# Plain attention: the maximum of a half is turned two periods sooner, and a third bank goes to turned tiles from period 9 on

## The reference

```python
energy = jnp.einsum('nhqd,nhkd->nhqk', q, k)
attn = jax.nn.softmax(energy / jnp.sqrt(jnp.float32(hd)), axis=3)
out = jnp.einsum('nhql,nhld->nhqd', attn, v)
```

## Time and profile before

| | us |
|---|---|
| median of 3 runs | 1981.02 (1980.35 to 1981.33) |
| the profiled execution | 1978.19 |
| its span, first to last instruction | 1976.4 |
| plain attention, first reduce to last output | 1011.4 to 1713 |
| reduces L1241, 512 | 590.8 busy |
| exponentials L1275, 1024 | 556.3 busy |
| turned tiles L1147, 1024 | 341.1 busy |

### The profile page before, as it was taken

The page is one execution under the profiler, slowest core; times in us unless marked ns, Lnnn a source line. Parts: engine busy times, 40 slices in busy tenths (PEclk is TensorE's granted clock), DMA queues, the critical chain, the costliest instruction groups (busy, mean ns, idle before and its releaser), DMA issues. The chain is left out here.

```text
span 1976.4 us, 40754 instructions
## 1 busy us (share of the span) xinstructions
PE 1741.5 (88%) x15061; PEld 901.7 (46%) x15061; DVE 1399.7 (71%) x3172; ACT 1151.1 (58%) x2314; POOL 581.1 (29%) x817
## 2 busy tenths in 40 slices
PE   5699999999999968799659999999999999687895
PEld 2356666666666545476312222222232332255563
DVE  6676766767788356542569999999899998656431
ACT  3336666666656632222328898989888887432231
POOL 2312122221122146677440000003310000167774
PEclk9779999999999978879768999999999998689888
DMA  5642744454540053232230000000000000062334
GB/s 162 162 84 50 129 90 78 96 98 72 92 89 12 23 150 60 34 59 36 77 127 9 28 18 18 24 29 18 18 18 24 28 3 23 17 171 38 60 40 84
DMA packets 108005, 120.95 MB, mean 61 GB/s; under 512 B 14360, under 2 KB 72960, under 8 KB 107808
## 3 DMA queue, kind: packets, MB, share of 16 engines
q1 hardware_dynamic: 83616, 100.97, 21.7%
q0 software_dynamic: 24192, 17.38, 6.4%
HBM read 81.71 MB, written 35.65 MB: 59 GB/s over the span
## 5 line engine op out<-in xcount | busy, mean ns | idle before, releaser
L1241 DVE TENSOR_REDUCE mx<-wide 128x2 f32<-128x1024 f32 x512 | 590.8, 1218 | 44.8 <-PE wide L1154 43.4
L1275 ACT ACTIVATE pT<-bank 128x512 f32<-128x512 f32 x1024 | 556.3, 595 | 89.5 <-PE bank L1147 79.1
L903 ACT ACTIVATE pT<-bank 128x512 f32<-128x512 f32 (+3 forms) x768 | 344.0, 490 | 238.8 <-PE bank L757 229.9
L1147 PE MATMUL bank<-q_st,k_st 51*128 51x512 bf16 x1024 | 341.1, 395 | 14.9 <-ACT pT L1275 7.6
L1154 PE MATMUL wide<-k_st,q_st 48*128 48x512 bf16 x1024 | 328.8, 400 | 23.8 <-DVE mx L1241 13.9
L1163 PE MATMUL bank<-pT,vst 128*32 128x256 f32 x4096 | 338.0, 403 | 0.0
L870 DVE TENSOR_REDUCE mx<-wide 128x1 f32<-128x640 f32 (+3 forms) x256 | 256.8, 1021 | 90.6 <-PE wide L772 86.5
L757 PE MATMUL bank<-q_st,k_st 122*128 122x512 f32 (+3 forms) x768 | 297.5, 397 | 6.9 <-ACT pT L903 5.0
L764 PE MATMUL wide<-k_st,q_st 120*128 120x512 f32 (+3 forms) x768 | 270.8, 370 | 20.3 <-PEq L371 11.7
L1860 POOL DMA_INDIRECT acc_rows<-yg,idx x128 | 201.9, 1577 | 102.0 <-DVE yg L2127 66.0
L1147 PEld LDWEIGHTS bank<-q_st,k_st 51*128 51x128 bf16 x1024 | 77.3, 94 | 260.2 <-ACT pT L1275 209.2
(11 more groups left out here) (328 smaller groups left out, 2008.6 us busy)
## 6 DMA issues: line engine op xcount, KB each, us to landing
q_st<-rope_split SPq DMA_DIRECT2D x60, 256.0 KB
k_st<-rope_split SPq DMA_DIRECT2D x60, 256.0 KB
qk_split<-parts SPq DMA_DIRECT2D x8, 1024.0 KB, 6.3
q_st<-qk_split SPq DMA_DIRECT2D x96, 64.0 KB
k_st<-qk_split SPq DMA_DIRECT2D x96, 64.0 KB
qk_parts<-parts SPq DMA_DIRECT2D x8, 768.0 KB, 4.6
xn_rows<-xn SPq DMA_DIRECT2D x8, 512.0 KB, 4.0
w1b<-in_L_ffn_w SPq DMA_DIRECT2D x16, 256.0 KB, 5.2
```

Source lines behind the costliest of these rows:

```text
L903: e.activation(pT[:, u % NPB, q0:HALF], bank[place_of[u]][:, q0:HALF], ACT.Exp, scale=scale).then_inc(s_p, 1)
L1147: e.matmul(bank[place_of[u]][:, :], k_st[at][64 * r:64 * r + KROW, jj, kc * P:(kc + 1) * P], q_st[at][64 * r:64 * r + KROW, jj, J * HALF:( ...
L1241: e.tensor_reduce(mx[G % 2][:, kh, pair:GH:2, c], wide[w % 2][:, :].rearrange("p (r k) -> p r k", r=2), AX.X, ALU.max).then_inc(s_sf, 1)
L1275: e.activation(pT[:, u % NPB, :], bank[place_of[u]][:, :], ACT.Exp, scale=scale).then_inc(s_p, 1)
```

## The change

The turning of a maximum moves from period 9 to period 7 on TensorE, ScalarE, GpSimd and SyncE alike, since all four ask `turns_max`. The bank's use `"max"` moves with it: the bank is taken in periods 6, 7, 8 and not in 8, 9, 10. So the third bank is given to tiles from period 9 on (9 periods, 18 tiles). Nothing is added or taken away.

```diff
             def turns_max(t):
 
-                G, at = divmod(t + LEAD - 4 - (NP - 1), NP)
+                G, at = divmod(t + LEAD - 2 - (NP - 1), NP)
                 return G if at == 0 and 0 <= G < 2 * STEPS else None
...
                 uses = [(NP * H + 3, NP * (H + 1) + 8, 2 + H % 2, ("out", H)) for H in range(2 * STEPS)]
-                uses += [(NP * G - 7, NP * G - 5, 2 + G % 2, ("max", G)) for G in range(2 * STEPS)]
+                uses += [(NP * G - 9, NP * G - 7, 2 + G % 2, ("max", G)) for G in range(2 * STEPS)]
                 uses += [(2 * NP * s + 14, 2 * NP * s + 19, 3, ("lent", s)) for s in LENT]
```

## The result

The kernel after takes 1973.91 us (median of 20 runs, 1967.80 to 1983.81). Beside it the kernel before took 1981.38 (20 runs, 1967.29 to 1988.30). The ratio is 0.9966, with a 95% interval of 0.9950 to 0.9983: faster by 0.34%.

What follows compares the result with a forecast made beforehand. A half was taken as a loop paced by VectorE, then TensorE. 23 ordinary halves x -0.02, six lent x 0.03 and the first half -0.2 gave -0.5 us: 1981.02 to 1980.5, range 1976.5 to 1983.5.

Steps and rivals of the forecast that it cites:

- The loop and its hand-overs: In each half VectorE's reduces pace period 5 to 2, TensorE 2 to 5; a score really waiting starts 0.06 after its reduce.
- I am wrong if: Signs: the gaps shrink together by over 0.1, L1223 waits for GpSimd, or a lent half grows by over 0.3.
- The gain that arrives in a half: Of some 0.22 us TensorE gains by period 11, 0.02 arrives at period 2's reduce; bounds 0 and 0.22.
- the segment from period 2 to 5: TensorE needs 4.66 us for these three periods, VectorE would need 3.39; banks there are the same as before.
- What the banks are worth in periods 9 and 10: With a third bank these periods needn't wait for the tile two before; another 0.05 us allowed.
- Lent halves: In six halves the bank goes in period 13, where the second tile waits: 0.03 to 0.23 us slower each, 0.03 likelier.
- the first half: TensorE is behind throughout and VectorE idles, so perhaps 0.2 us arrive, once.
- The end: From 1661.20 on, clock 0.67, TensorE busy 45.36 of 52.40 us: more banks and the moved maximum change nothing.
- The range: 1976.5 to 1983.5, from clock dips of some 3 us costing 1.3 to 1.5 each; chance within 0.80.
- All of TensorE's gain arrives: Rival: scores of periods 10 to 2 don't wait for reduces; 30 halves 0.22 shorter, -6.6, 1974.4; chance 0.11.
- The maximum comes too soon: Slower rival: in period 7 TensorE reaches the turn before GpSimd's split is ready; +9, 1990; chance 0.06.
- the gaps are for want of banks: Rival: the third bank removes both VectorE gaps (periods 4, 5), 0.80 us in 30 halves; -24, 1957; chance 0.02.

Runs made afterwards that it cites:

- the turn alone: Before with the maximum turned in period 7 but the third bank still kept from tiles until period 11: 1979.22 us, 0.9995; again on another chip 1949.41, 1.0008.
- the unchanged kernel: The kernel before timed against itself, nothing changed: 1979.77 us against 1979.72, 0.9999; again on another chip 1949.47, 1.0021.
- all but the last half: Before with the change in every half except the last: 1978.93 us, 0.9994; later 1954.37, 1.0038, and 1977.03, 0.9977.
- the last half alone: Before with the change only in the last half: 1974.76 us, 0.9975; later 1976.75, 0.9979, and 1976.64, 0.9988.
- the third comparison: Runs on a chip where before took 1947.82 us: before unchanged 1.0021, change in every half but the last 1.0038, turn moved without the bank 1.0008, more banks 1.0003.
- the one with more banks still: The changed kernel, with last-stretch tiles also allowed one half of each wide bank: 1948.96 us, 1.0003 against before.
- the pair with the long stop: `BEGIN` one period sooner, so TensorE waits a period more: in before 1983.39 us, 1.0013; with the change in the last half 1983.71, 1.0019.
- the changed kernel with the later `BEGIN`: The changed kernel with the router's late steps starting one period later (`LAST - LEAD + 2`): 1973.52 us, 0.9963 against before.

## Why the prediction was wrong

**The loop and its hand-overs: right.** VectorE sets the pace from the reduce of period 5 to period 2 and TensorE from there to period 5; the scores of periods 8 to 2 start 0.05 to 0.06 behind their reduces, the two gaps are still there, L1223 starts 0.32 behind the split's end, and GpSimd and SyncE delay nothing. None of the three signs named as "I am wrong if" appeared.

**The gain that arrives in a half: 0.068, not 0.02.** The mis-sized term is the segment from period 2 to 5. It was taken as fixed, since its banks don't change. But the second tile of period 2 waits for an exponential and not for the reduce, and stands 1.56 behind the first tile of period 1 in both kernels. In before TensorE was catching up, at 1.11 us a period; in after it goes with VectorE at 1.13, and the first tile of a period no longer starts with the score but 0.02 to 0.03 ahead of it. So the exponentials run 0.05 ahead in relation to the score: 0.45 becomes 0.40. With the 0.02 of the hand-over this makes 0.07, as measured. It is well inside the bounds of 0 to 0.22.

**What the banks are worth in periods 9 and 10: wrong.** The 0.05, "a guess that no row separates", is too small: the turn alone moved nothing, so with two banks TensorE is late in period 10 by as much as with the turn. In the result this changes nothing, as both parts are made together.

**Lent halves: right; the first half: not shown.** A lent half went from 21.97 to 22.02, +0.05 where 0.03 was taken from 0.03 to 0.23. That holds for the four in the middle; the last has 22.06 to 22.07 in both kernels, and the first differs by 1 us between traces of the same kernel. In the two profiled executions the first half went from 20.94 to 20.71 where -0.2 stood. But in two others, the unchanged kernel and all but the last half, in which the clock came back 2 us sooner, it is 20.22 with the change and without.

**The sum of these:** 23 x -0.068 + 4 x 0.05 = -1.4 us, and -1.6 with the 0.23 of the first half, where -0.5 was predicted. The kernel with all halves changed but the last shows -2.2 ± 1.1. This alone would have been inside the range, at about 1979.5.

**The end: the step that failed.** The prediction put the last stretch at nothing; changed in its last half alone, the kernel was 4.0 ± 0.8 us faster. "More banks for tiles don't help, and the maximum only changes its place among TensorE's work" was an argument from a share, 45.36 of 52.40 us busy at a clock of 0.67. The share was itself a consequence of the clock: where it doesn't fall, the same 25 us have TensorE busy for 22.05 and not 24.44, with a fifth more matmuls. Real work saved there is about 0.35 us (periods 487 to 497 take 13.84 in the profiled execution of after and 14.19 in that of the unchanged kernel, both at the full clock). The rest of the last half's 4.0 us comes with 16 us fewer at the lower clock. This much the pooled executions show, the last half alone on three chips and after on two of these and more; on the chip of the third comparison the one kernel with the last half's change (the one with more banks still) was no faster than before. How the edit brings it about is not shown: the lengths above support a sooner recovery without proving it, and the pair with the long stop doesn't show it. Nor is it shown that it is the bank and not the place of the turn, which in the last half moves into the period of the stop: the turn alone, at 1978.0 ± 1.4 and 312.5 us, lies between before and the last half alone. That stays open.

**The range.** It allowed the clock ±3 us, at 0.43 to 0.5 us for each us at the lower level; the executions show 0.316. Its row was misread: the reduce at 1048.67 is one of period 5, which stands 1.70 behind the one ahead at the full clock too (1089.54 - 1087.84), so 1.98 against 1.13 compares two different periods. The range rested besides on a median of three runs that lay within 1 us. The executions of before in the later comparisons lie between 1965 and 1989 (without the third), and of that spread three runs so close to one another had said nothing. But the range failed for the missing 4 us, not for the spread, since medians of 20 stand side by side.

**The rivals.** "All of TensorE's gain arrives" named 1974.4, and the time came out at 1973.9. That is luck, for its mechanism is false: it wanted 0.22 in each of 30 halves, and they gave 0.068. "The maximum comes too soon" and "the gaps are for want of banks" did not occur: there is no wait for GpSimd, and both gaps are there. By the Trainium skill (Perfetto Trace Analysis, Identifying Performance Opportunities) a repeating gap can mean too little PSUM; the gap of period 4 gave way by 0.07 and that of period 5 by nothing, so the trace doesn't bear it out here.

**A better version?** None is shown. The changed kernel with the later `BEGIN` has 1973.9 ± 0.8 and the changed kernel 1973.5 ± 0.7; they ran on different chips, and in the one comparison that has both, the former is 2.4 us lower by the median, within the noise. The wider choice of banks was never timed beside the changed kernel.

## What to carry to other kernels

A loop that changes hands between two engines gains only what arrives at the hand-over, and of the segment behind it each wait has to be followed, not only the first. Where the trace shows the granted clock low in a stretch, the clock can be worth more than the work in the change (here about 4 us against 0.35): price such a stretch at both levels before it is put at nothing. And where the clock varies from execution to execution, take dozens of runs and split the change, since neither one trace nor one comparison tells 0.2% from none.

## What the runs showed of the hardware

- Behind one idle time of TensorE of about 1 us the granted clock fell to 1.2 GHz in ten of 16 traces, and in some and not in others of the same kernel, and stayed there for 3.4 to 44.4 us. It didn't fall there in two traces without that stop, and it did in two with a longer one. The mean of before was 3.7 ± 1.1 us lower without the stop and 2.4 ± 1.0 higher with the longer one, in one comparison each.
- One us at the lower clock costs 0.316 us over this kernel's executions. Rows of the last stretch agree: three of its periods take 2.21 + 1.67 + 1.55 = 5.43 us at the lower level and 1.74 + 1.00 + 0.96 = 3.70 at the full one, and (5.43 - 3.70) / 5.43 = 0.32.
- Four chips ran the same kernel in 1980 to 1982 us (medians) and a fifth in 1948. Identical kernels differed by 0.01% in one comparison and by 0.21% in another, whose interval of 0.04 to 0.38% leaves out zero.
